# New orders of work on every engine in stage one of a one-core attention and expert kernel

## The reference

```python
def attn(out, W_write, W_read, decay, log_alpha):   # 4 heads of 64, decayed linear attention
    gamma = sigmoid(decay)
    v  = out @ W_write.T                            # per head
    rk = out;  wk = out shifted by one token
    # by chunks: inter = (W rk) * gamma**p;  intra = ((rk wk^T) * M) v
    #            W_new = gamma**C * W + (v * gamma**(C-1-p))^T wk
    reads = alpha * (inter + intra)
    return out + reads @ W_read.T

def ffn(x, gate_w, w1, b1, w2, b2):                 # 8 experts, the best 2 of each token
    probs = softmax(x @ gate_w.T);  topk_probs, topk_idx = top_k(probs, 2)
    h = gelu(x @ w1[expert] + b1[expert])           # 256 -> 1024
    y = h @ w2[expert] + b2[expert]                 # 1024 -> 256
    return sum(y * topk_probs)

x = x + attn(layernorm(x), ...)
x = x + ffn(layernorm(x), ...)
```

## Time and profile before

| what | value |
|---|---|
| median of 3 runs | 578.55 us (577.62 to 579.43) |
| the profiled execution's own time | 580.98 us |
| its span, first to last instruction | 579.2 us |
| mean granted TensorE clock | 0.974 of full speed |
| TensorE matmuls busy | 537.9 us, 93% of the span |
| VectorE busy | 458.0 us, 79% |
| ScalarE busy | 333.2 us, 58% |
| GpSimd busy | 241.5 us, 42% |

### The profile page before, as it was taken

One profiled execution on the slowest core, in us unless ns is written; L12 is line 12 of the kernel. 1 busy time (PEld: TensorE's weight loads), 2 busy tenths in 40 slices (PEclk: granted clock), 3 DMA queues, 4 the chain that ended last, 5 costly groups with the idle time before them and its releaser, 6 DMA issues.

```text
span 579.2 us, 17638 instructions
## 1 busy us (share of the span) xinstructions
PE 537.9 (93%) x5246; PEld 422.4 (73%) x5246; DVE 458.0 (79%) x1408; ACT 333.2 (58%) x841; POOL 241.5 (42%) x275
## 2 busy tenths in 40 slices
PE   8689899898889978999999999999999999999991
PEld 7567777777767746777777777777777777777770
DVE  6889998899867799868778777777777877777771
ACT  6799989788735833455555445444545454545540
POOL 2415777588754652423332223333323332223332
PEclk9989999799889999999999999999999999999996
DMA  5667766566333564344333444444444433444422
GB/s 175 218 203 227 221 213 218 170 212 224 110 104 94 132 175 80 59 75 69 64 61 66 70 76 75 76 76 73 66 70 67 65 61 63 68 74 76 75 49 27
DMA packets 85097, 63.34 MB, mean 109 GB/s; under 512 B 54224, under 2 KB 77392, under 8 KB 85008
## 3 DMA queue, kind: packets, MB, share of 16 engines
q1 hardware_dynamic: 71328, 43.94, 29.9%
q0 software_dynamic: 13392, 18.27, 17.2%
q10 hardware_dynamic: 288, 0.00, 0.0%
HBM read 37.56 MB, written 24.62 MB: 107 GB/s over the span
## 4 chain that ended last, share of the span: by engine, by line
PE 67%; DVE 14%; POOL 7%; issue 7%; ACT 2%; another core or an unknown queue 1%; DMA 1%; DVEq 0%; ACTq 0%; POOLq 0%
PE psum L1512 30%; PE psum L1527 20%; PE psum L1529 10%; POOL sent_rows L495 3%; PE psum L1332 2%; DVE arena L909 2%; DVE weights L773 2%; POOL tiny L485 1%; DVE tiny L852 1%; PE psum L1422 1%; POOL tiny L482 1%; DVE arena L845 1%; PE psum L1415 1%; DVE arena L920 1%
## 5 line engine op out<-in xcount | busy, mean ns | idle before, releaser
L1512 PE MATMUL psum<-arena,weights 128*128 128x256 f16 (+1 forms) x2208 | 279.4, 249 | 1.2 <-DVE arena L1134 0.8
L1512 PEld LDWEIGHTS psum<-arena,weights 128*128 x2208 | 187.9, 98 | 78.7 <-issue 2.6
L731 ACT ACTIVATE arena<-psum,b_cur 128x256 f32<-128x256 f32 (+1 forms) x368 | 131.8, 424 | 161.7 <-PE psum L1512 127.5
L1527 PE MATMUL psum<-weights,arena 128*128 x568 | 215.4, 380 | 5.0 <-DVE arena L1142 4.5
L526 POOL DMA_INDIRECT out<-arena,tile_in x71 | 114.9, 1619 | 248.9 <-DVE arena L1155 152.2
L1529 PE MATMUL psum<-weights,arena 128*128 x568 | 155.1, 273 | 0.0
L1142 DVE TENSOR_TENSOR arena<-arena 128x512 f16<-128x512 f32 x142 | 99.6, 701 | 4.9
L495 POOL DMA_INDIRECT sent_rows<-arena,tiny x64 | 65.8, 1028 | 28.6 <-issue 16.9
L1140 DVE CAST arena<-arena 128x512 f16<-128x512 f32 x142 | 61.5, 433 | 8.4 <-ACT arena L731 7.7
L1527 PEld LDWEIGHTS psum<-weights,arena 128*128 128x128 f16 x568 | 55.7, 98 | 12.1 <-issue 6.1
L1529 PEld LDWEIGHTS psum<-weights,arena 128*128 128x128 f16 x568 | 55.7, 98 | 4.7
(11 more groups left out here) (172 smaller groups left out, 646.3 us busy)
## 6 DMA issues: line engine op xcount, KB each, us to landing
weights<-in_experts SPq DMA_DIRECT2D x32, 512.0 KB, 4.5
arena<-sent_rows SPq DMA_DIRECT2D x100, 64.0 KB
arena<-in_b SPq DMA_DIRECT2D x46, 128.0 KB
arena<-in_x SPq DMA_DIRECT2D x16, 256.0 KB, 3.2
out<-arena SPq DMA_DIRECT2D x16, 256.0 KB
arena<-sent_rows SPq DMA_DIRECT2D x84, 32.0 KB
sent_rows<-pad SPq DMA_DIRECT2D x7, 265.0 KB
tile_in<-sent_rows SPq DMA_DIRECT2D x71, 4.5 KB
```

What stands on the lines that cost most here:

```text
L731: last = a.activation(act[:, g % 2, m * n:(m + 1) * n], ps_h[:, g % 2, m * n:(m + 1) * n], ACT.Gelu_apprx_tanh, scale=1.0 / WSCALE, bias=b ...
L1512: last = pe.matmul(ps_h[:, f % 2, mm * n:(mm + 1) * n], w1_of(e_of[i], k, lo, per * (f - GROUP[i]) + mm), turned[:, i % 2, part, k, 0:n], ...
L1527: pe.matmul(to, h_hi[:, z % 4, at], w2_of(e_of[t], m), start=(m == 0), stop=(m == MF - 1), skip_group_check=True)
```

## The change

It leaves the arithmetic as it is and moves work within stage one.
- SyncE: from step 5 on the weight loads of the next step are issued after the store of the step, the first when TensorE has finished `weigh` of chunk n-2 (`score_ps`), the others when it has finished `reads` of it (`read_ps`).
- GpSimd: the same instructions in the same order, written as functions.
- ScalarE: the first high half opens the step; the second comes after `exponential`, ahead of `normed_transposed` and `chunk_keys`; the others come later. It also takes over the copy of the expert scores (`logits`) from VectorE in steps 4 to 17.
- VectorE: `largest` first, `chunk_queries` after `weigh_scores`, `residual` before `carry`; from step 7 on both remainders come at the end of the step, right behind `place`.
- TensorE: `weigh` before `values`, and `states` last in the step, after `reads`.

```diff
--- before.py
+++ after.py
@@ -55,6 +55,8 @@
 AHEAD = 2
 LAG = 5
 ROWS = 4
+PACED = 5
+ROUTED = 6
 PIECES = (0, 0, 1, 4, 3, 3, 3, 2, 2, 2, 2, 2, 2, 2, 2, 2)
 assert sum(PIECES) == NPIECE
 NE = 4
@@ -389,8 +391,9 @@
                 par = n % 2
                 if active(n + 1, 0) and n > 0:
                     load_x(n + 1, 1 - par)
-                for j in splits(n + 1):
-                    load_piece(j)
+                if n < PACED:
+                    for j in splits(n + 1):
+                        load_piece(j)
                 if n == 3:
 
                     sp.wait_ge(setup_pool, 3)
@@ -413,6 +416,10 @@
 
                         reached(sp, "res_done", m + 2)
                     sp.dma_start(both(out, m), res_of(m)).then_inc(x1_out[1 - par], 16)
+                if n >= PACED:
+                    for j, passed in zip(splits(n + 1), ("score_ps", "read_ps", "read_ps")):
+                        reached(sp, passed, n - 2)
+                        load_piece(j)
 
             def load_rows(i):
 
@@ -466,35 +473,50 @@
             pool.memset(pad[:], 0.0).then_inc(setup_pool, 1)
             pool.wait_ge(setup_pool, 1)
 
+            def norm(m, moments, ve, rs, shift, got, mid, end, last, used, ago):
+
+                reached(pool, got, m)
+                reached(pool, used, m - ago - 1)
+                pool.tensor_scalar(ve, moments[:, :, 1], EPS, None, ALU.add)
+                pool.tensor_scalar(shift, moments[:, :, 0], -1.0, None, ALU.mult).then_inc(S[mid], 1)
+                reached(pool, mid, m)
+                pool.tensor_tensor(rs, ve, minus_half[:].to_broadcast([P, B]), ALU.pow).then_inc(S[end], 1)
+                reached(pool, end, m)
+                pool.tensor_tensor(shift, shift, rs, ALU.mult).then_inc(S[last], 1)
+
+            def norm_chunk(m):
+
+                s = m % 2
+                norm(m, moments1, ve1, rs1[s], shift1[s], "moments1_done", "ve1_done", "rs1_done", "shift1_done",
+                     "res_done", 1)
+
+            def norm_residual(m):
+
+                norm(m, moments2, ve2, rs2, shift2, "moments2_done", "ve2_done", "rs2_done", "shift2_done",
+                     "xm_done", 0)
+
+            def send(m, b):
+
+                if m == 0:
+                    pool.wait_ge(setup_dve, 18)
+                for name in ("token_done", "xm_done", "gates_done", "slot_i_done"):
+                    reached(pool, name, m)
+                for k in range(2):
+                    at_bk = slot_i[:, m % ROWS, 2 * b + k:2 * b + k + 1]
+                    pool.indirect_dma_start(
+                        out=sent, out_offset=bass.IndirectOffsetOnAxis(ap=at_bk, axis=0),
+                        in_=row[:, m % ROWS, b, :], in_offset=None).then_inc(row_out[m % ROWS], 16)
+
             def step(n):
 
...
+                if active(n, 0):
+                    norm_chunk(n)
+                if active(n, 3):
+                    norm_residual(n - 3)
+                if active(n, LAG):
+                    send(n - LAG, 0)
+                if active(n, LAG):
+                    send(n - LAG, 1)
@@ -660,6 +682,12 @@
                 a.activation(xnT[:, 0, s, :, :, P:P + 1].rearrange("p b k t -> p (b k) t"), src,
                              ACT.Copy).then_inc(S["xcol_done"], 1)
 
+            def logits(m):
+
+                reached(a, "logit_ps", m)
+                reached(a, "top_at_done", m - 1)
+                a.activation(logit, ps_logit, ACT.Copy).then_inc(S["logit_done"], 1)
+
             def chunk_residual(m):
 
                 s = m % 2
@@ -672,32 +700,36 @@
 
             def step(n):
 
+                for j in splits(n)[0:1]:
+                    split_high(j)
                 if 1 < n <= NCH + 1:
                     last_column(n - 1)
                 if active(n, 1):
                     chunk_high(n - 1)
-                for j in splits(n)[0:1]:
-                    split_high(j)
                 if active(n, 1):
                     chunk_residual(n - 1)
                 if active(n, 5):
                     exponential(n - 5)
+                for j in splits(n)[1:2]:
+                    split_high(j)
+                if active(n, 4):
+                    normed_transposed(n - 4)
                 if 1 <= n < NCH:
                     chunk_keys(n - 1)
-                for j in splits(n)[1:2] if len(splits(n)) > 2 else ():
-                    split_high(j)
                 if active(n, 2):
                     chunk_values(n - 2)
-                if active(n, 4):
-                    normed_transposed(n - 4)
-                for j in splits(n)[2:] if len(splits(n)) > 2 else splits(n)[1:]:
-                    split_high(j)
                 if active(n, 0):
                     chunk_normalise(n)
+                for j in splits(n)[2:3]:
+                    split_high(j)
                 if n == NCH + 1:
                     high_tile(0)
+                if active(n, 4):
+                    logits(n - 4)
                 if active(n, 3):
                     normalise(n - 3)
+                for j in splits(n)[3:]:
+                    split_high(j)
                 if active(n, 2):
                     reads_high(n - 2)
 
@@ -925,28 +957,26 @@
 
                 if n == NCH:
                     early_count()
+                if active(n, 5):
+                    largest(n - 5)
                 if active(n, 0):
                     chunk_stats(n)
                 if active(n, 5):
-                    largest(n - 5)
-                if active(n, 3):
-                    carry(n - 3)
+                    choose(n - 5)
                 if active(n, 0):
                     moments(n)
-                if active(n, 5):
-                    choose(n - 5)
                 if active(n, 1):
                     chunk_low(n - 1)
                 if n == NCH + 1:
                     reached(v, "xcol_done", NCH - 1)
                     v.tensor_copy(xnT[:, 1, (NCH - 1) % 2, :, :, P:P + 1].rearrange("p b k t -> p (b k) t"),
                                   zcol[:]).then_inc(S["xlo_done"], 1)
-                if active(n, 1):
-                    chunk_queries(n - 1)
                 if active(n, 3):
                     residual(n - 3)
-                for j in splits(n)[0:1]:
+                for j in splits(n)[0:1] if n <= ROUTED else ():
                     split_low(j)
+                if active(n, 3):
+                    carry(n - 3)
                 if active(n, 3):
                     residual_stats(n - 3)
                 if active(n, 5):
@@ -957,14 +987,16 @@
                     turn(0)
                 if active(n, 2):
                     weigh_scores(n - 2)
+                if active(n, 1):
+                    chunk_queries(n - 1)
                 if active(n, 5):
                     place(n - 5)
-                if active(n, 4):
-                    logits(n - 4)
                 if n == NCH + 1:
                     low_tile(0)
                 if n == NCH:
                     early_table()
+                for j in splits(n)[0:1] if n > ROUTED else ():
+                    split_low(j)
                 for j in splits(n)[1:]:
                     split_low(j)
 
@@ -1445,17 +1477,17 @@
                 if active(n, 4):
                     turn_normed(n - 4)
                 if active(n, 2):
+                    weigh(n - 2)
+                if active(n, 2):
                     values(n - 2)
-                if active(n, 2):
-                    weigh(n - 2)
                 if active(n, 5):
                     rank(n - 5)
-                if 2 <= n <= NCH:
-                    states(n - 2)
                 if active(n, 4):
                     score_experts(n - 4)
                 if active(n, 2):
                     reads(n - 2)
+                if 2 <= n <= NCH:
+                    states(n - 2)
 
             pe.wait_ge(setup_dve, 1)
             keep_warm(96)
```

26 lines of the change are left out of this document (removed).

## The result

The changed kernel takes 588.17 us (median of 4 runs, 586.01 to 592.02) against 578.99 for the kernel before (4 runs): a ratio of 1.0142, with an interval of 1.0107 to 1.0177. It is slower by 1.4%, and the forecast was 572.4. One thing is needed to read what follows. The later runs were made in five groups, each on a chip of its own, and the kernel before has one of two levels in a group: 569.4, 569.7 and 570.1 us in three of them ("the low level"), 579.9 and 582.1 in two, and 579.0 in this first comparison ("the high level"). No chip was used for two groups, so it is not shown whether the level belongs to the chip or to the time of the runs. The traces ahead of the prediction are of the high level.

The account below looks back on a forecast made before the run. Stage one's steps were taken as bound by GpSimd, stalled behind VectorE's remainders. Gains of 3.5 (steps 7 to 15), 1.9, 0.2 and 0.5 sum to 6.1 us, median 578.55 to 572.4; own range 570 to 576, full range 567.0 to 580.5.

Parts of the forecast that it names:

- The one stall of 1.89 us of step 10: VectorE's wait for no instruction of the profile in step 10; kept once, 1.9 us, without the slow step behind it.
- The fourth rival: Stage one: two waits like step 10's return, each with a slow step (1.9 + 2.2 us); 578.8 us; chance 0.13.
- each of the nine steps loses 1.0 us on average to something else: Steps 7 to 15: 10.30 us each against 9.30 in step 12, mainly from GpSimd's norms stalling behind two remainders.
- The paced loads, 5.5 + T: Steps 7 to 15: loop of 5.5 us plus weight load time T, taken as 4.2, makes the step 9.7 us.
- VectorE's floor of 9.2 us: Steps 7 to 15: VectorE's own work, 9.30 us less 0.08 for the scores' copy, sets 9.2 us a step.
- GpSimd's 9.3: Steps 7 to 15: 5.98 us from slots to last send plus two norm chains of 1.66 make 9.3 us.
- The stalls gone: GpSimd, steps 7 to 15: stalls of 2.0 us a step vanish if the second norm ends before the slots.
- the sends 0.96 to 1.35: GpSimd's sends beside two remainders in a row take 0.96 to 1.35 us; a sign that the forecast is right.
- Rival 3, the lockout: GpSimd can't write DMA descriptors while remainders run: 10.8 us a step in steps 7 to 15, 580.5 us; chance 0.04.
- The high half ahead of `chunk_high`: ScalarE: 0.94 us placed where VectorE waited, covered by other work; priced at nothing, 0.94 a step as a bound.
- Steps 3 and 4, 1.9 us: VectorE's waits in step 4 for `chunk_high` and the projection go as norm and reads come sooner: gain 1.9 us.
- Steps 16 on, 0.5 us: Steps 16 and 17: `weigh` before `values` gives VectorE its scores earlier, saving its wait in step 16: 0.5 us.

Follow-up runs that it names:

- the unpaced kernel: Changed kernel with weight loads issued as before, ahead of the store with no wait for TensorE: 0.9920, 0.9913, 0.9914 (low level), 1.0147 (high) against the kernel before.
- the third group: 19 extra matmuls (about 1.1 us) ahead of the transposes of chunks 4 to 14: kernel before 1.0296, changed 1.0595, changed with loads as before 1.0590.

## Why the prediction was wrong, step by step

- *The step that failed: "The one stall of 1.89 us of step 10 I keep once, without the slow step behind it, as TensorE has fewer gaps to fall into."* At the high level seven of the nine steps of the changed kernel have late signals (11 waits), and in steps 10 to 14 the granted clock was 0.77 to 0.95. The nine steps took 14.9 us more than in the same kernel without late signals (101.8 less 86.9), 11.9 in a second pair of traces (99.0 less 87.1), where the prediction put 1.9. TensorE's busy time grew by 8.0 us of the 14.9 (88.6 less 80.6), mostly the slower clock; the rest is waiting. That TensorE "has fewer gaps" did not keep the signals away. The fourth rival had this mechanism, priced at two waits with a slow step each, 8.2 us. The rest of the term was right: 9 x 9.7 is 87.3, and 86.9 came without late signals, so the miss in the nine steps is this one term.
- *The base of the comparison, "each of the nine steps loses 1.0 us on average to something else", with GpSimd named as that something.* The same kernel takes 86.8 us for them at the low level, stalls and all. So of the 9.0 us above nine steps of 9.3, 5.9 went with the level. They lie where late signals are: steps 10, 11, 13, 14 and 15 took 11.7, 11.5, 10.3, 10.3 and 10.95 us, where a step at the low level takes 9.75 from step 8 on. In the trace of the kernel before one shows as the "remote" wait of step 10; those of steps 13 to 15 show as waits of 0.47, 0.49 and 1.11 us on the projection, which I read as its own length. It had ended 0.7 to 1.4 us before the residual started (the last of the three below), and 0.2 us before it at the low level. The two steps of 10.3 us from which the prediction took GpSimd's bound are of these, and so was the first stall of 1.0 us. Nor was the 9.30 of step 12 an undisturbed step of this kernel: that is 9.75. The stalls, taken away by themselves, gave 0.06 us a step.

```profile
147.70 1.99 PE L1332 MATMUL psum<-wrT,arena 128*128 128x256 f32 x8 [0.62 <-ACT arena L637]
...
151.06 0.69 DVE L845 TENSOR_TENSOR arena<-psum,arena 128x512 f32<-128x512 f32 x1 [1.11 <-PE psum L1332]
```

- *The paced loads, 5.5 + T.* The loop is right: 10.2 us with the measured T of 4.7, and steps of 10.0 to 10.2 were there; T of 4.2 was too small by 0.5. But not each step is bound by it, and at the low level the nine took 86.9 and 87.1 us, where 9 x 9.7 is 87.3. So this term of the sum was met by luck, by two errors that cancel. What it hid is that pacing costs all of what the new orders gain there: 83.2 without it. In the medians that is 0.35 to 0.5% (0.9914 against 0.9949; 0.9913 against 0.9962); the intervals touch or overlap, but the two groups agree.
- *VectorE's floor of 9.2 us and GpSimd's 9.3.* VectorE's is right: 9.21 us a step in the low-level traces of the unpaced kernel. GpSimd's 9.3 was 0.1 too long, as it kept up with 9.21. *The stalls gone, the sends 0.96 to 1.35:* right. Rival 3, the lockout: did not happen.
- *Moving the first remainder.* Within the new orders it is worth about 1%: 1.0065 with it in the middle, in one group, against 0.9962 and 0.9949 for the changed kernel in two others. In the old orders it is worth 0.1%.
- *The high half ahead of `chunk_high`, "I price this at nothing".* At the low level right: 0.9928 with it second against 0.9914, intervals that overlap. At the high level no run separates it.
- *Steps 3 and 4, 1.9 us.* Met in the first pair (34.27 against 36.16). Over eleven traces of kernels with all the new orders up to that step, the residual of step 4 starts at 34.2 to 36.5, mean 34.8; in five of the old orders at 35.7 to 36.5, mean 36.1. So 1.3 on average. In the first pair step 6 gave it back: ScalarE waited 1.2 us for a paced load and VectorE 1.2 for a late signal.
- *Steps 16 on, 0.5 us.* 2.0 in the first pair. At the low level the stretch from the end of step 15 to the first expert matmul is 20.8 us in the kernel before and 20.1 and 20.2 in the changed one: 0.6 to 0.7. The 3.24 us wait of the earlier trace rows, kept as it was, was of the late kind too: there is no such wait in the low-level traces.

What is shown and what isn't. Shown: both kernels run without late signals at the low level and the change is a gain of 0.4 to 0.5% there; at the high level it is a loss of 1.1 to 1.4%, and of 1.5% without pacing, and the loss lies in the nine steps, in which late signals and slow-clock stretches stand. That the late signals are the whole of it is argued from the traces: no run took them away on a chip that has them. That the new orders have less slack for a late TensorE is what the third group supports (before lost 17 us to the added work, changed and unpaced 26), but the added work raised the number of late signals too, so slack and number are not separated. Which of the new orders does it is open. TensorE's old order, unpaced, gave 1.0061 at the high level against 1.0147 for the new one, but on another chip, and its nine steps (63.59 to 161.79 in VectorE's timeline) took 98.2 us, no less than the 98.4. That kernel has only 3.5 us of late signals in three steps and is no faster for it, so the length of the nine steps does not follow from the sum of these waits alone. Open too is what holds TensorE's signals up, and why one group of runs has it and another does not. Of the edits only the changed and the unpaced kernel ran at both levels, and neither is faster than the kernel before at both. Unpaced is the best at the low one (0.991 to 0.992) and among the slowest at the high one.

## What to carry to other kernels

Look for waits that end with no instruction of the profile, and for waits on an instruction that had ended a microsecond before, and set them apart in the base of the sum before any stall is priced: here 5.9 of the 9.0 us that seemed to be for the taking went with them. A stall on one engine is worth only what the next bound leaves: 1.4 us of stalls a step gave 0.06 when taken away alone. And a schedule that runs an engine at 99% of a step leaves no room for a late signal: run such a change on more than one chip before keeping it.

## What the runs showed of the hardware

The same kernel took 569.4 to 570.1 us on three chips and 580 to 582 on two others, and a change of 1% or less had the opposite sign at the two levels (0.995 and 0.996, 1.011 and 1.014). The difference is not in stage one alone: in the kernel before, 12.0 us lie between the two profiled executions (579.2 and 567.2), 5.9 of them in the nine steps, 3.0 from there to the first expert matmul and 2.9 from that to the last one, in code that the change does not touch (382.0 us against 379.1; the changed kernel 381.9 and 382.2 against 379.4 and 379.6). In stage one it shows as late signals of TensorE: none between 20 and 200 us in the low-level traces of the unedited kernels, 15 of them in the changed kernel's first trace (21.6 us together, up to 4.0 each). In steps 8, 9, 10, 13 and 17 of that trace TensorE itself pauses too (0.16 to 1.18 us), and two or three engines resume within 0.1 us; at the two late signals to `last_column` and in step 15 no pause of TensorE shows. The weight loads are no slower at the high level: 3.6, 4.5 and 5.2 us there and 3.7, 4.4 and 6.1 at the low one for the kernel before. The second cost is the granted clock: over the nine steps it was 1.00 in four of the five low-level traces read so and 0.98 in the fifth, and at the high level 0.96 in the kernel before and 0.92, 0.93 and 0.98 in the changed and the unpaced one, falling to 0.57 right behind the waits (0.50 with the extra matmuls).
